# A new beginning by batch, and a new end with the expert products in the base's banks, in a fused attention and LoRA-expert kernel

## The reference

```python
x = L0_attn_hidden_states                       # (2, 512, 512)
xn = _layernorm(x, axis=-1)
x = x + attn(xn, qkv_w, out_w, gate_w, norm_w) + ffn(xn, W_base, b_base, W_router, A, B)

# attn: 32 heads of 128, blocks of 32 positions, a decay per head
qkv = silu(hidden_states @ qkv_w.T)
scores = einsum('bhnd,bhmd->bhnm', cq, ck) * diag_decay          # within a block
kv_next = kv * block_decay + einsum('bhnd,bhne->bhde', ck * k_decay, cv)
xf = xf * rsqrt(mean(xf * xf) + EPS)                             # over all heads of a token
return sigmoid(hidden_states @ gate_w.T) * (norm_w * xf) @ out_w.T

# ffn: 8 experts of rank 16, the best two of each token
probs = softmax(x_flat @ W_router.T); topk_probs, topk_idx = top_k(probs, 2)
topk_probs = topk_probs / sum(topk_probs)
h = einsum('nd,erd->ner', x_flat, A); hw = h * combine[:, :, None]
out = x_flat @ W_base.T + b_base + einsum('ner,eor->no', hw, B) * 2
```

## Time and profile before

| what | us |
|---|---|
| time, median of 3 runs | 1158.83 (1156.89 to 1160.56) |
| the profiled execution, its own time | 1157.6 |
| its span, first to last instruction | 1155.8 |
| PE busy in the span | 1090.5 (94%) |
| DVE, ACT, POOL busy | 727.8, 688.8, 642.2 |
| mean granted PE clock | 0.984 of full speed |

### The profile page before, as it was taken

One profiled execution on the slowest core, in us unless ns is written; L12 is line 12 of the kernel. 1 busy time (PEld: TensorE's weight loads), 2 busy tenths in 40 slices (PEclk: granted clock), 3 DMA queues, 4 the chain that ended last, 5 costly groups with the idle time before them and its releaser, 6 DMA issues. The chain is left out here.

```text
span 1155.8 us, 18941 instructions
## 1 busy us (share of the span) xinstructions
PE 1090.5 (94%) x5848; PEld 946.0 (82%) x5848; DVE 727.8 (63%) x1212; ACT 688.8 (60%) x1401; POOL 642.2 (56%) x629
## 2 busy tenths in 40 slices
PE   2669989999999999999999999999999999999985
PEld 2458878988889888988889888988889888988974
DVE  5646747566665767566656757575666757465646
ACT  5636746566566756566656756576556756575520
POOL 3644865448473765458473755457473756367420
PEclk9879999999999999999999999999999999999989
DMA  6230411111010211011020211011020211011021
GB/s 210 79 115 4 165 64 46 38 42 60 24 60 18 78 40 52 30 41 59 23 76 1 82 36 64 18 41 59 23 77 2 86 35 59 19 42 60 26 98 73
DMA packets 41973, 64.23 MB, mean 56 GB/s; under 512 B 3920, under 2 KB 21328, under 8 KB 41424
## 3 DMA queue, kind: packets, MB, share of 16 engines
q1 hardware_dynamic: 41648, 63.73, 17.2%
q10 hardware_dynamic: 288, 0.03, 0.0%
HBM read 54.84 MB, written 8.91 MB: 55 GB/s over the span
## 5 line engine op out<-in xcount | busy, mean ns | idle before, releaser
L391 POOL TENSOR_TENSOR w_lo<-combo,w_hi 128x768 fp32r<-128x768 f32 (+1 forms) x132 | 171.7, 1309 | 167.2 <-ACT w_hi L531 167.0
L391 POOL TENSOR_TENSOR w_lo<-raw,w_hi 128x256 fp32r<-128x256 f32 (+1 forms) x132 | 133.8, 1016 | 134.5 <-ACT w_hi L531 134.1
L1068 DVE TENSOR_TENSOR acc<-acc,outp 128x512 f32<-128x512 f32 x120 | 82.2, 685 | 76.4 <-PE outp L1352 75.3
L1350 PE MATMUL bank_q<-t_hi,w_hi 128*128 128x512 f32 x288 | 116.0, 403 | 10.2 <-ACT ys L531 4.7
L434 POOL TENSOR_TENSOR sum_sq<-sum_sq,square 128x512 f32<-128x512 f32 x64 | 82.9, 1296 | 73.8 <-ACT square L667 73.8
L1352 PE MATMUL bank_q<-t_hi,w_lo 128*128 128x512 f32 x288 | 113.9, 396 | 0.0
L1351 PE MATMUL bank_q<-t_lo,w_hi 128*128 128x512 f32 x288 | 113.8, 395 | 0.0
L1350 PE MATMUL outp<-wo_hi,g_hi 128*128 128x512 f32 x256 | 102.9, 402 | 9.1 <-DVE g_lo L1052 4.7
L964 DVE TENSOR_TENSOR xs<-bank_r,xs 128x512 f32<-128x512 f32 x66 | 45.6, 691 | 99.7 <-ACT xs L531 71.0
L1020 DVE TENSOR_TENSOR score<-score,table 128x512 f32<-128x512 f32 (+1 forms) x128 | 75.9, 627 | 42.4 <-PE score L1352 42.3
L1352 PE MATMUL outp<-wo_hi,g_lo 128*128 128x512 f32 x256 | 102.3, 400 | 0.0
(11 more groups left out here) (195 smaller groups left out, 3396.9 us busy)
## 6 DMA issues: line engine op xcount, KB each, us to landing
raw<-w_chunks SPq DMA_DIRECT2D x165, 256.0 KB, 2.9
table<-near_dram SPq DMA_DIRECT2D x32, 128.0 KB, 2.0
near_dram<-near_b SPq DMA_DIRECT2D x3, 1024.0 KB, 5.1
acc<-x SPq DMA_DIRECT2D x8, 256.0 KB, 6.0
acc<-x SPq DMA_DIRECT2D x2, 1024.0 KB, 6.4
xb_dram<-acc SPq DMA_DIRECT2D x2, 1024.0 KB, 5.3
y<-xb_dram SPq DMA_DIRECT2D x2, 1024.0 KB, 7.1
out<-acc SPq DMA_DIRECT2D x8, 256.0 KB, 2.1
```

The lines of the kernel that those rows point to most:

```text
L391: pool.tensor_tensor(piece(w_lo[i % 2], j), piece_source(i, j), piece(w_hi[i % 2], j).bitcast(F32), ALU.subtract).then_inc(wlo[j], 1)
L1068: dve.tensor_tensor(tile, tile, outp, ALU.add).then_inc(acc_done, 1)
L1350: pe.matmul(out_, a_hi, b_hi, start=start, stop=False, skip_group_check=True)
```

## The change

**The beginning.** The two LAST units are replaced by `first_rows(r, b)`: a plain product of one row of weights (q, k and two gates, r = 0 to 3) with the tokens of one batch b, 12 matmuls of 512 columns for each, 96 in all where 84 stood. Batch 0 begins when its four tiles are split, before batch 1 is normed. The layer norm is in two halves. Weights for these rows are split by POOL alone (`split_first`). The tokens' tiles are split straight from the transposes' banks; the combinations stand in `acc`, which is free then, and the SBUF that the decay tables use is that of the combinations' hi and lo, so that these wait until the tables are stored in HBM. The choice of experts is made shorter (a tanh of the gap of the two best logits in place of a softmax) and is moved into body 0, to the places where output tiles -4 to -1 stand in the other bodies, and so are the turning of h and the store to `hw_dram`.

**The end.** The experts' products are added into the base's banks p, q and r ahead of products 2, 3 and 4; only those that would belong to the x tile are made into `score`. `hw` and B are loaded and split early in the last body. `y` is loaded in eight pieces. The last four outputs use `outp` and `bp` in turn, and the final result of batch 1 is made straight from the bank.

**The loop.** A few places on ACT, DVE and POOL are exchanged; PE's order is the same. In the last body PE has `prod(QK0, 6)` ahead of `scores(6)` and `output(8)` ahead of `prod(QK0, 3)`.

```diff
@@ SP @@
-            unit_taken(0, LAST + QK0)
+            sp.wait_ge(first_wlo, 1)
             load_v(0, 0, 1, 11, 1)
...
-            sp.wait_ge(turned, NTB)
+            sp.wait_ge(t_lo_done, 3)
+            sp.wait_ge(t3_lo_done, 1)
             sp.dma_start(base_b, b_base.rearrange("(a h) -> a h", a=1).to_broadcast([P, HID])).then_inc(bias_in, 16)
             sp.dma_start(acc[:, TB:, :], x_tok[:, 0:TB, :]).then_inc(xb_in[0], 16)
-            sp.wait_ge(hwt_done, 2)
-            sp.dma_start(hw_dram, hw_t).then_inc(hw_out, 16)
...
                 if first:
+                    sp.wait_ge(hwt_done, 2)
+                    sp.dma_start(hw_dram, hw_t).then_inc(hw_out, 16)
                     sp.wait_ge(xb_done, 1)
                     sp.dma_start(xb_dram[:, 0:TB, :], acc[:, TB:, :]).then_inc(xb_out, 16)
...
                 unit_taken(g, QK3)
+                if final:
+
+                    sp.wait_ge(hw_out, 16)
+                    sp.dma_start(raw[0][:, :, :].rearrange("p a n -> p (a n)"), hw_dram).then_inc(raw_in[0], 16)
+                    sp.wait_ge(hwlo_done, 1)
+                    sp.dma_start(raw[0][:, 0:2, :], w_chunks[FFN_B:FFN_B + 1].rearrange("a p (c n) -> (a p) c n", c=2)).then_inc(raw_in[0], 16)
+                    sp.wait_ge(btlo_done, 1)
                 load_rows(0, 20 * g + 18, 20 * g + 19)
@@ POOL @@
+            def split_first(u):
+                pool.wait_ge(raw_in[u], 32)
+                pool.tensor_copy(first_hi[:, u], raw[u][:]).then_inc(first_whi, 1)
+                pool.wait_ge(first_whi, u + 1)
+                pool.tensor_tensor(first_lo[:, u], raw[u][:], first_hi[:, u].bitcast(F32), ALU.subtract).then_inc(first_wlo, 1)
 
             combine, low = weights(0)
...
+            power(1, slice(0, TB))
+            split_first(0)
+            power(2, slice(TB, NTB))
@@ DVE, in body 0 @@
+                early = {-4: two_best, -3: weigh_experts, -2: lambda: keep_hw(0), -1: lambda: keep_hw(1)}
+
...
+                        early[t]()
@@ DVE, the loop @@
+                make_u2(G23)
                 make_c12(QK2)
-                make_u2(G23)
                 far_of(2)
                 add_out(1)
+                gate_att(3)
                 lo(QK2, "r")
-                gate_att(3)
@@ PE @@
+            def first_rows(r, b):
+
+                pe.wait_ge(first_wlo, r // 2 + 1)
+                pe.wait_ge(xl_done, TB * b + TB)
+                if b == 1:
+                    pe.wait_ge(first_low if r < 2 else first_gate, r % 2 + 1)
+                for kc in range(KC):
...
+                    mm = three(first_bank[r], first_hi[:, r // 2, at, w], first_lo[:, r // 2, at, w], hi, lo, kc == 0, kc == KC - 1)
+                mm.then_inc(first_ready, 1)
...
+            for t in range(TB):
+                turn_tokens(t)
+            first_rows(0, 0)
+            first_rows(1, 0)
+            first_rows(2, 0)
+            for t in range(TB, NTB):
+                turn_tokens(t)
+            first_rows(3, 0)
             pe.wait_ge(ar_in, 16)
-            pe.wait_ge(xt_done, 3)
...
+                if base and m in (2, 3, 4):
+                    pe.wait_ge(hwlo_done, 1)
+                    pe.wait_ge(btlo_done, 1)
+                    for t in range(2):
+                        expert(banks[b][:, t * 256:t * 256 + 256], TB * COL[b] + 2 * pair + t, ROW[b], False)
...
+                        last = t - 12 if final else -1
+                        to = bp if last >= 0 and last % 2 else outp
+                        if last < 1:
+                            at_least(pe, acc_done, 16 * g + t)
+                        elif last == 1:
+                            pe.wait_ge(free["p"], unit(g, G01) + 1)
+                        else:
+                            pe.wait_ge(last_done, last - 1)
```

More of the change, by code:

```diff
@@ L83, in weights_in @@
 def weights_in(g, i):
-    return 32 if i < 0 else raw_full(g, RAW_OF[i])
-RAW_OF = {LAST + QK0: 0, LAST + G01: 1, V1: 0, V2: 1, QK1: 2, QK2: 3, G23: 5, QK3: 6, QK0: 7, G01: 9, NEXT + V1: 10, NEXT + V2: 11}
+    return raw_full(g, RAW_OF[i])
+RAW_OF = {V1: 0, V2: 1, QK1: 2, QK2: 3, G23: 5, QK3: 6, QK0: 7, G01: 9, NEXT + V1: 10, NEXT + V2: 11}
 RAW_WO = (4, 8)
@@ L613, in body, with copy_m1 @@
             def body(g, first=False, final=False):
-                copy_m1, copy_u2, copy_u3, silu_, whole_, hi_, gate_, weight_ = units(g)
+                copy_m1_, copy_u2, copy_u3, silu_, whole_, hi_, gate_, weight = units(g)
+                def copy_m1(i):
+                    if first and i == V2:
+                        act.wait_ge(route, 1)
+                        act.activation(gap[:], gap[:], ACT.Tanh, scale=0.5).then_inc(route_act, 1)
+                    copy_m1_(i)
                 def silu(i, c):
-                    if not (final and i == QK0):
+                    if not (first and i < 0):
@@ L764, in body @@
                 gate(G23, "p")
+                weight(QK3, 4)
+                copy_u2(G23)
                 silu(QK2, "r")
-                copy_u2(G23)
                 whole(QK2, "r")
-                weight(QK3, 4)
+                squares(3)
                 hi(QK2, "r")
-                squares(3)
                 copy_u3(G23)
@@ L900, in _ @@
-            silu(LAST + QK0, "p")
-            whole(LAST + QK0, "p")
-            hi(LAST + QK0, "p")
-            silu(LAST + QK0, "x")
-            silu(LAST + QK0, "q")
-            whole(LAST + QK0, "q")
-            hi(LAST + QK0, "q")
-            whole(LAST + QK0, "x")
+            for t in range(3):
+                tokens_whole(t)
+            first_q(0)
+            tokens_whole(3)
+            first_k(0)
+            weight(V1, 2)
+            tokens_hi(4)
+            tokens_hi(5)
@@ L918, in _ @@
-            copy_u2(LAST + G01)
-            copy_u3(LAST + G01)
-            weight(V2, 2)
-            gate(LAST + G01, "x")
-            gate(LAST + G01, "q")
-            gate(LAST + G01, "p")
-            weight(V2, 3)
-            for t in range(2):
-                act.wait_ge(hw_turned, t + 1)
-                copy(hw_t[:, 512 * t:512 * t + 512], score[:, t, :]).then_inc(hwt_done, 1)
-            act.wait_ge(near_out, 64)
+            first_gates(0, 0)
+            weight(V2, 2)
+            act.wait_ge(near_out, 32)
@@ L1068, in add_out, with add_base @@
                         dve.tensor_tensor(tile, tile, outp, ALU.add).then_inc(acc_done, 1)
+                def add_base(i, c):
+                    u = i - QK0
+                    if c == "p" or c == "q":
+                        dve.wait_ge(m_done[2 if c == "p" else 4], unit(g, i) + 1)
+                    else:
+                        dve.wait_ge(c22_made if c == "x" else c12_made, unit(g, i) + 1)
+                    dve.wait_ge(y_in[COL[c]][u], 32)
+                    part = y[COL[c]][:, 2 * u:2 * u + 2, 256 * ROW[c]:256 * ROW[c] + 256]
+                    dve.tensor_tensor(part, banks[c].rearrange("p (t n) -> p t n", t=2), part, ALU.add).then_inc(free[c], 1)
@@ new lines, in inverse_root, with scaled, result @@
+                def inverse_root(b):
+                    refine(3 + b, slice(TB * b, TB * b + TB))
+                def scaled(t, of, more):
+                    return dve.scalar_tensor_tensor(out=acc[:, t, :], in0=of, scalar=rs[:, 1, t:t + 1], in1=more, op0=ALU.mult, op1=ALU.add)
+                def result(t):
+                    dve.wait_ge(acc_done, 16 * g + NTB + t + 1)
+                    for c in "pq":
+                        dve.wait_ge(free[c], unit(g, QK0 + t // 2) + 1)
+                    scaled(t, acc[:, t, :], y[0][:, t, :]).then_inc(result_done, 1)
@@ L1381, in prod @@
                     for m in ms:
-                        product(g, i, m, by_token=i in (V1, V2) or (final and i >= QK0))
+                        if first and i == V1 and m == 5:
+                            pe.wait_ge(first_gate, 3)
+                        product(g, i, m, by_token=i in (V1, V2) or (final and i >= QK0), base=final and i >= QK0)
                 def scores(s):
@@ new lines, in rms @@
+                def rms(b):
+                    pe.wait_ge(summed, STEPS * SGS - 1 + b)
+                    pe.wait_ge(plo2_done, STEPS * SGS)
+                    if b == 1:
+                        pe.wait_ge(pow_ready, 3)
+                    for t in range(TB):
+                        mm = pe.matmul(score23[:, TB * b + t:TB * b + t + 1], sum_sq[:, b, t * P:t * P + P], ones[:],
+                                       start=True, stop=True, skip_group_check=True)
+                    mm.then_inc(rms_ready, 1)
```

1083 lines of the change are left out of this document (744 added, 339 removed).

## The result

The changed kernel takes 1121.3 us (median of 4 runs, 1119.8 to 1121.6) against 1158.4 (4 runs, 1156.9 to 1160.6): ratio 0.9669, 95% interval 0.965 to 0.9689. Forecast were 1129 and a range of 1117 to 1142. The profiled execution took 1121.6 with a span of 1119.8, 36.0 less than the 1155.8 of before. In the experiments further down, medians and ratios leave out two slow executions, one of e5 (1969.3 us) and one of the kernel before (2791.4).

The account below looks back on a forecast made before the run. PE was taken as full in the middle, with gains only from waits at both ends: beginning -26.2, body 0 +2.5, +1.0 and +7.0, loop 0, end -15.2, +1.0, sum -29.9 on 1157.6: 1127.7, as median 1129; range 1117 to 1142.

Parts of the forecast that it names:

- the chain of DVE and POOL behind the eighth tile: Beginning: normings, splits and last lo parts ready at 56.3, so body 0 starts at 57, a gain of 24.2 us.
- PE's own chain: Beginning: last split at 21.1, then 34.2 us of PE work kept fed, so done at 55.3.
- a warmer clock: Start of body 0: PE enters warm, and 2.0 us lost before at the lower clock are gained.
- SP's chain: Body 0: hw_dram's store delays x's store and load, POOL's addition, later weights and PE's product 7 of G23: +7.0 us.
- the routing: Body 0: two groups of eight linked DVE operations choosing experts delay make_u2(V2), make_c22(V2) and ACT: +2.5 us.
- the exchange: Loop: lo(QK2,"r") moves behind gate_att(3), costing nothing with 0.8 us of slack; 0.7 a body without PE's cover.
- y's share: End: y asked for seven us sooner removes PE's 4.7 us wait and 2.4 lost to the clock behind it.
- the banks': End: last four outputs alternating between two banks remove 4.4 us of PE waits; 1.5 more lost to the cooled clock.
- Rival 1: Body 0: second load of x in time or later weights hidden by PE's work, the +7.0 falls away: 1122; chance 0.15.
- Rival 2: Body 0 and beginning: DVE's small operations each wait for a POOL operation: 1140, or 1138 by the skill's rule; chance 0.17.
- Rival 3: End: y or G01's weights still late, PE stops again for 5 us and cools: 1137; chance 0.11.
- rival 4: Loop: gate_att(3) waits long and bank r is free late in every body, making it slower: 1163; chance 0.03.

Follow-up runs that it names:

- e5: Changed kernel with the choice of experts later in body 0: first group behind make_u2(V2), second behind make_c22(V2), multiplications behind lo(V2,"x"); 1121.6 us, ratio 0.9678.
- e2: e1 with the second store of x plus bias also moved behind the load of the next weights and the table; 1111.5 us, ratio 0.9595.
- e4: Changed kernel with SP asking for y only after POOL has split the second half of the output weights; 1122.2 us, ratio 0.9693.
- e9: Changed kernel with y asked for as late as in the kernel before, in one load for each batch; 1127.5 us, ratio 0.9733.
- e11: Changed kernel with the first product waiting until all eight tiles are transposed, ACT's and DVE's lists changed to match; 1129.7 us, ratio 0.9759.
- e1: Changed kernel with the hw_dram store placed behind the load of the second half of x in SP's body 0 list; 1114.7 us, ratio 0.9618.
- e10: e2 with the choice of experts moved: first group behind make_u2(V2), second behind lo(V2,"p"), multiplications behind make_c22(V2); 1107.4 us, ratio 0.9574.
- e13: Changed kernel with DVE doing lo(QK2,"r") ahead of gate_att(3) again, as in the kernel before; 1120.2 us, ratio 0.9668.
- e3: Changed kernel with all of the last four output tiles in the one bank outp, each behind the result before; 1125.1 us, ratio 0.9708.
- e7: Changed kernel with SP's eight output stores issued in the order in which DVE makes the results; 1118.2 us, ratio 0.9651.
- e6: Changed kernel with POOL's first subtraction of 1024 columns waiting until DVE has normed the first tile; 1121.4 us, ratio 0.9678.
- e12: e2 with e10's routing, e7's stores, result(1) right behind result(0), and POOL's first subtraction held until four tiles are normed; 1103.4 us, ratio 0.9531.

## Why the prediction came out as it did

The forecast was right in sign and in where the time would go and come from, wrong on what bounds the beginning, and 7.7 us high by the medians. By the span, -29.9 was forecast and -36.0 measured. The difference of 6.1 comes from three terms.

**The beginning, -24.2 forecast, -27.9 measured: too small by 3.7.** The step that was mis-sized is the choice of the bound. I took the chain of DVE and POOL behind the eighth tile at 56.3 and rounded it to 57; it ended at 51.8, and PE's own chain set the start at 53.27. That one I had put at 55.3, 21.1 for the last `b_lo` and 34.2 of work; measured were a first matmul at 19.77 and 33.5. The 1.3 us at its start come from one guess: a cast and a subtraction of 1024 columns at 2.4 each, where the cast took 1.04 (the subtraction 2.34). The 2.4 us for a slow first dozen were 2.0 in this execution and nothing in those of e2, e4 and e9, so how near this sum comes is in part luck. That PE is kept fed, which I only assumed, held: it has no wait from 19.77 until body 0 is under way. e11 shows how much of the gain is the early first product: with it behind all eight tiles 7.1 us of the start are gone. What the other 20.8 us consist of is read from the waits of both kernels and was not undone by a run.

**Body 0, +10.5 forecast less 2.0 for a warmer clock, +5.1 measured: 3.4 less.** SP's chain was right link by link: hw's store at 103.5 (50.2 behind the body's start, 49 forecast), POOL held, the weights and ACT late, PE idle ahead of product 7. The term that was mis-sized is its price. Without it, in e1, the stretch to product 7 is 69.9 us, so the chain cost 4.7 and not 7.0, and all the rest together 0.4 (69.9 for 69.5) where I had 1.5. I had POOL's second addition 7.2 later than before; measured from the start of body 0 it came 6.2 later (61.2 for 55.0), because the load of x landed 5.5 us behind its issue, where I had used 6.4. The weights behind it then took 6.0 us from issue to ACT's use and not 6.8 as before, so ACT came 5.3 later and PE 5.1. In the rest, the routing was put at +2.5: its stall was 1.90, and it was worth 2.4 to 4.1 in e10. The two groups of transposes took 0.35 each, 0.7 together, where I had 1.0. What I had not seen is that the chain had a second half worth some 3 us more (e2 against e1: 3.1 by the medians, 2.7 by the ratios, 2.9 in the stretch to product 7): the second store stands ahead of the weights in the kernel before too.

**The loop, 0 forecast,** was 0, and e13 shows that it does not depend on the exchange.

**The end, -14.2 forecast, -13.2 measured** (from product 7 on, the loop included). The waits went as described. e9 gives y's share as 6.2 to 7.4 (I had 4.7 and 2.4 for the clock), e3 the banks' as 3.8 to 4.5 (I had 4.4 and 1.5). The tail beyond PE is longer than forecast, 8.2 us and not 7.5 (PE's last matmul ends at 1111.6): five stores stand behind the last result, and e7 shows that their order in SP's list costs 2 to 3 us.

**The rivals.** Rival 1 (SP's chain hidden, 1122) has the right number for a wrong reason: the chain cost its 5 us, and two other terms were too careful. A time alone would have spoken for it; the rows at 108.95 to 127.87 and e1 do not. Rival 2 (DVE's small operations each wait for POOL) did not happen in body 0: of the sixteen linked operations two took more than 0.23 us (0.65 and 0.49). POOL ran only two operations of 0.7 us beside them (at 67.67 and 70.61), and the two long ones ended with these; so the argument against this rival, that POOL waits for ACT's weights there, held. The block itself is real: 2.20 us in the refinement, and 4.33 for a copy of 4 columns beside `add_bias(0)`. What it meets is decided by where POOL's long operations stand, as e5 and e6 show. The Trainium skill, "SBUF — State Buffer", section "Who interferes with whom", names two-input operations in SBUF and the copies and `tensor_scalar` forms of the two-port modes as those that can be blocked, and says that reductions never are. By that rule the traces agree: those blocked are a copy, a `tensor_scalar` and two-input operations in SBUF, and `v_lo` from a PSUM bank took 0.41 to 0.42 where the one from `xs` took 3.75. The reductions among the linked operations met no POOL operation in the changed kernel; in e5 one did and took 0.22, where the two-input operation right behind it took 1.53, until POOL's ended. Rival 3 (the end gives less) fell, since PE has no wait over 0.3 us there; rival 4 fell with the full loop and e13.

## What to carry to other kernels

When a store that waits for late work moves in a DMA engine's list, price the loads behind it and not the store: here one misplaced wait ahead of a chain store, load, add, store, weights cost 5 to 6 us, and the same reading gave 3 more in a place that the change never touched. The block between DVE and POOL did not go away by a small move (e6); look for a stretch in which DVE works from PSUM, as in e12, where its splits beside POOL's subtraction took no longer than with POOL idle (1.27 us for two). And a wait removed in the profile is not worth what DVE stood there: in e4 5.7 us of it cost PE 1.4 of waiting, in e9 3.8 us more cost PE 3.3 more, and the time was 5.3 higher than in e4 (4.6 by the ratios).

## What the runs showed of the hardware beyond that

- On POOL a cast of 128x1024 took 1.04 us and the subtraction of the same size 2.34, and the pair for the second half of the weights 1.04 and 2.38.
- A copy of 4 columns on DVE took 4.33 us beside a POOL addition of 2048 columns (4.77), and ended with it.
- PE's first matmuls differ between executions of the same beginning. In the changed kernel the first nine full-width matmuls took 0.63 to 0.76 us and came 0.43 apart (0.56 behind the first), the later ones 0.39 to 0.40 and 0.23 apart. In e2, e4 and e9, whose beginning is the same and in which PE also stood idle for 1.50 to 1.65 us just ahead, the first took 0.47 and the next 0.39 to 0.40; in e5 all of the first twelve were slow. 0.43 apart is also what the matmuls behind product 7 have, at a granted clock of 0.50, but in the beginning the clock's column says 1.00, so the rows do not show that this was the clock.
- In e11 the first matmul took 0.48 and the next 0.39 us, with four tiles transposed from 26.46 to 30.5 right ahead of them. As e2, e4 and e9 have the same without these transposes, they are not needed for it; what decides it stays open.
- So the start of body 0 moves without an edit: it came at 51.83 to 54.37 in the ten profiled executions that share the changed kernel's beginning (the changed kernel, e1 to e5, e7, e9, e10, e13).
